# An adaLN block with windowed attention and 8 experts: rows sorted batch by batch, 13 of 39 expert tiles inside attention's drain

## What is computed

```python
mod = (_silu(L0_c) @ L0_wmod).reshape(L0_c.shape[0], 6, 1, -1)
h = _layernorm(x, axis=-1) * (1 + ca) + sa
x = x + ga * attention(h)          # 16 heads of 8, query block of 128 sees keys within +-128
h = _layernorm(x, axis=-1) * (1 + cb) + sb
router_logits = h @ gate           # [2048, 8]
routing_weights, selected = top_k(router_logits, 2); routing_weights = softmax(routing_weights)
eo[e] = (silu(h @ w1[e]) * (h @ w3[e])) @ w2[e]      # w1, w3: 128x512, w2: 512x128
x = x + gb * sum over the 2 selected experts of weight * eo[e]
```

## Time and profile before

| | us |
|---|---|
| median of 3 runs | 348.94 (348.21 to 350.21) |
| the profiled execution's own time | 349.13 |
| its span, first to last instruction | 347.3 |
| TensorE busy | 277.7 |
| VectorE busy | 227.4 |
| ScalarE busy | 184.9 |
| GpSimd busy | 180.6 |
| mean granted clock of TensorE | 0.917 |

### The profile page before, as it was taken

One profiled execution on the slowest core, in us unless ns is written; L12 is line 12 of the kernel. 1 busy time (PEld: TensorE's weight loads), 2 busy tenths in 40 slices (PEclk: granted clock), 3 DMA queues, 4 the chain that ended last, 5 costly groups with the idle time before them and its releaser, 6 DMA issues. The chain is left out here.

```text
span 347.3 us, 6884 instructions
## 1 busy us (share of the span) xinstructions
PE 277.7 (80%) x2281; PEld 204.6 (59%) x2281; DVE 227.4 (65%) x573; ACT 184.9 (53%) x406; POOL 180.6 (52%) x269
## 2 busy tenths in 40 slices
PE   3568799999998999999854056999999999999200
PEld 2134354555554555555333035999999999999200
DVE  5657978888888799887437893555555555554064
ACT  7432477757675766667710104556665555555050
POOL 4130245456655475657650125477777777775221
PEclk9999999999999999999985555999999999999855
DMA  3942332544647372300000001011111121112283
GB/s 93 175 69 60 71 100 53 175 133 141 183 109 213 73 236 67 105 1 19 17 15 16 0 0 40 23 48 54 47 47 46 53 49 46 47 46 40 78 218 92
DMA packets 36243, 26.89 MB, mean 77 GB/s; under 512 B 4088, under 2 KB 31752, under 8 KB 36208
## 3 DMA queue, kind: packets, MB, share of 16 engines
q1 hardware_dynamic: 32368, 20.48, 21.5%
q0 software_dynamic: 2496, 5.12, 5.6%
q10 hardware_dynamic: 1344, 0.86, 1.4%
HBM read 15.41 MB, written 4.67 MB: 58 GB/s over the span
## 5 line engine op out<-in xcount | busy, mean ns | idle before, releaser
L819 DVE TENSOR_REDUCE negm<-psA 128x4 f32<-128x1024 f32 x64 | 78.2, 1223 | 14.2 <-PE psA L1141 13.1
L428 ACT ACTIVATE probs<-psB 128x512 f32<-128x512 f32 x128 | 71.1, 593 | 21.4 <-PE psB L1163 21.1
L589 POOL TENSOR_SCALAR_AFFINE_SELECT probs<-probs 128x512 f32<-128x512 f32 x64 | 39.1, 634 | 42.2 <-ACT probs L428 42.2
L700 POOL DMA_INDIRECT y_d<-kd,sca_idx x39 | 45.3, 1162 | 22.9 <-ACT kd L497 22.9
L1297 PE MATMUL psA<-kd,probs 128*128 128x128 f32 x416 | 53.1, 284 | 0.0
L1297 PEld LDWEIGHTS psA<-kd,probs 128*128 128x128 f32 x416 | 51.1, 201 | 0.0
L1138 PE MATMUL psA<-kd,qs 96*128 96x512 bf16 x128 | 47.6, 395 | 1.7 <-DVE negm L819 1.5
L695 POOL DMA_INDIRECT kd<-h_d,gat_idx x39 | 38.2, 980 | 18.5 <-PE psO L1289 9.8
L1163 PE MATMUL psB<-qs,kd 98*128 98x256 bf16 x256 | 45.1, 273 | 1.5 <-ACT probs L428 1.0
L1307 PE MATMUL psM<-probs,kd 128*128 128x128 f32 x312 | 41.3, 275 | 0.4 <-ACT kd L497 0.4
L1307 PEld LDWEIGHTS psM<-probs,kd 128*128 128x128 f32 x312 | 37.9, 192 | 0.6 <-DVE kd L1030 0.6
(11 more groups left out here) (185 smaller groups left out, 402.6 us busy)
## 6 DMA issues: line engine op xcount, KB each, us to landing
w_sb<-in_L_ffn_experts_w_dram SPq DMA_DIRECT2D x12, 512.0 KB, 4.8
kd<-parts SPq DMA_DIRECT2D x96, 32.0 KB
qs<-parts SPq DMA_DIRECT2D x42, 64.0 KB
mod_sb<-mod_d SPq DMA_DIRECT2D x8, 320.0 KB, 5.0
probs<-y_d SPq DMA_DIRECT2D x8, 256.0 KB, 5.0
h_d<-h SPq DMA_DIRECT2D x8, 128.0 KB, 1.9
out_dram<-probs SPq DMA_DIRECT2D x4, 256.0 KB, 2.3
x_sb<-in_L_attn_x_dram SPq DMA_DIRECT2D x1, 640.0 KB, 9.6
```

Source lines behind the costliest of these rows:

```text
L428: nc.scalar.activation(probs[:, kt, n % PRING], psB[:, kt, :].rearrange("p (h q) -> p h q", h=H2), ACT.Exp).then_inc(s["exped"], 1)
L589: nc.gpsimd.affine_select(out=u, in_=u, compare_op=ALU.is_ge, fill=0.0, base=0, pattern=[[0, 2 * H2], [-sign, P]], channel_multiplier=sign ...
L700: pool.indirect_dma_start(y_d, bass.IndirectOffsetOnAxis(ap=sca_idx[:, n:n + 1], axis=0), ys[:, r], None).then_inc(scattered[r], 16)
L819: nc.vector.tensor_reduce(negm[:, b % 2, :, :, j], psA[:, n % 2].rearrange("p q (h k) -> p q h k", h=H2), AX.X, ALU.max, negate=True).then ...
```

## The change

- Each pair of token and expert gets its row as soon as its batch is routed. xs_d holds a region of 2176 rows for each expert: 128 blanks, then its rows in order of arrival. A row is 130 words: h2, the row of y_d for its result, and its weight. `place_rows` (VectorE) takes the ranks that `rank_rows` (TensorE) makes for two token blocks, and `put_rows` (GpSimd) writes 128 rows with one indirect DMA, four for a batch. This takes the place of the one-hot inverse and of the gathers.
- After batch 4 is routed, `early_list` makes a list of 13 tiles (NEARLY), each full and inside its region; after batch 7 `late_list` makes the other 26, counted back from each region's end.
- Steps 9 to 11 are gone. What was left of batches 5, 6 and 7 is written between the turns of the first tiles. Scatter 13 waits for the six scatters before it.
- SyncE loads a tile's rows with a plain DMA (`load_xs`, ring of 5, a slot being free when its scatter has landed) and w2 of the tile's expert from DRAM (`load_w2`); w2 is no longer held in SBUF. psG and psU have two buffers, not three.
- y_copy multiplies by the row's weight, and y_d is laid out by partition (`(k p t) c`), so that the combine is a sum.

```diff
+                sp.dma_start(pay[:, b % PAYRING, 1, :, 0:C], pay[:, b % PAYRING, 0, :, 0:C]).then_inc(h2_copied[b % PAYRING], 16)
+            def load_w2(n):
+                if n >= TRING:
+                    sp.wait_ge(s["y_ps"], n - TRING + 1)
+                e = sp.value_load(tile_e[0:1, bass.ds(n, 1)], min_val=0, max_val=E - 1)
+                sp.dma_start(w2_t[:, n % TRING].rearrange("p (k c) -> p k c", c=C),
+                             w2[bass.ds(e, 1)].rearrange("e (k p) c -> p (e k) c", p=P)).then_inc(w2_in[n % TRING], 16)
+            def load_xs(n):
+                if n >= XRING:
+                    sp.wait_ge(*result_down(n - XRING))
+                row = sp.value_load(tile_row[0:1, bass.ds(n, 1)], min_val=0, max_val=XROWS - P)
+                sp.dma_start(xs[:, n % XRING], xs_d[bass.ds(row, P), :]).then_inc(xs_in[n % XRING], 16)
...
+            sp.wait_ge(s["list_ready"], 2)
+            sp.wait_ge(s["scoresB"], 2 * NPAIR * B)
+            for n in range(TRING):
+                load_w2(n)
+            for done, count in xs_put_by(EB):
+                sp.wait_ge(done, count)
+            for n in range(XRING):
+                load_xs(n)
+            copy_h2(B - 2)
+            for n in range(NTILE):
+                if n + TRING < NTILE:
+                    if n + TRING == NEARLY:
+                        sp.wait_ge(s["list_ready"], 4)
+                    load_w2(n + TRING)
+                if n + XRING < NTILE:
+                    if n + XRING == NEARLY:
+                        sp.wait_ge(s["list_ready"], 4)
+                        sp.wait_ge(s["blanked"], 32)
+                        for done, count in xs_put_by(B):
+                            sp.wait_ge(done, count)
+                    load_xs(n + XRING)
+                if n == 2:
+                    copy_h2(B - 1)
...
+            y_t = y_d[0:TOPK * NTOK].rearrange("(k p t) c -> p k t c", k=TOPK, p=P)
             for i in range(4):
                 for k in range(TOPK):
                     sp.dma_start(y01[:, k, n * i:n * i + n], y_t[:, k, n * i:n * i + n]).then_inc(s[f"y_in{i}"], 16)
...
+            def put_rows(b, k, t):
+                r = b % PAYRING
+                pool.wait_ge(s["dest_ready"], 3 * b + 3)
+                if k == 1:
+                    pool.wait_ge(h2_copied[r], 16 * (b // PAYRING + 1))
+                pool.indirect_dma_start(xs_d, bass.IndirectOffsetOnAxis(ap=dest[:, b, k, t:t + 1], axis=0),
+                                        pay[:, r, k, t], None).then_inc(xs_put[r], 16)
...
             def scatter(n):
-                r = n % TRING
...
+                if n == NEARLY:
+                    for m in range(NEARLY - YRING, NEARLY):
+                        pool.wait_ge(*result_down(m))
                 pool.wait_ge(s["y_ready"], n + 1)
-                pool.indirect_dma_start(y_d, bass.IndirectOffsetOnAxis(ap=sca_idx[:, n:n + 1], axis=0), ys[:, r], None).then_inc(scattered[r], 16)
-            for n in range(TRING):
-                gather(n)
-            pool.wait_ge(s["xsT_first"], 1)
-            gather(TRING)
+                pool.indirect_dma_start(y_d, bass.IndirectOffsetOnAxis(ap=xs[:, n % XRING, C:C + 1].bitcast(I32), axis=0),
+                                        ys[:, n % YRING], None).then_inc(scattered[n % YRING], 16)
+            put_rows(3, 1, 1)
+            put_rows(4, 0, 0)
+            pad_term(B - 1)
+            put_rows(4, 0, 1)
+            x1_sum(B - 2)
+            put_rows(4, 1, 0)
+            ln2_rstd(B - 2)
+            put_rows(4, 1, 1)
+            h2_scale(B - 2)
+            h2_shift(B - 2)
             for n in range(NTILE):
-                if n + TRING + 1 < NTILE:
-                    pool.wait_ge(s["xsT_ps"], n + 1)
-                    gather(n + TRING + 1)
+                if n == 1:
+                    weights_pow(B - 3)
+                if n == 2:
+                    ln2_rstd(B - 1)
+                if n == 3:
+                    put_rows(B - 3, 0, 0)
+                if n == 4:
+                    weights_pow(B - 2)
+                    put_rows(B - 3, 0, 1)
+                if n == 5:
+                    weights_pow(B - 1)
+                    put_rows(B - 3, 1, 1)
+                if n == 6:
+                    put_rows(B - 2, 0, 1)
+                if n == 7:
+                    put_rows(B - 2, 1, 1)
+                if n == 8:
+                    put_rows(B - 1, 0, 1)
+                if n == 9:
+                    put_rows(B - 1, 1, 1)
                 scatter(n)
+                if n == 4:
+                    put_rows(B - 3, 1, 0)
+                if n == 5:
+                    put_rows(B - 2, 0, 0)
+                if n == 6:
+                    put_rows(B - 2, 1, 0)
+                if n == 7:
+                    put_rows(B - 1, 0, 0)
+                if n == 8:
+                    put_rows(B - 1, 1, 0)
...
+            def mix(b):
+                tt, r = slice(2 * b, 2 * b + 2), b % PAYRING
+                dve.wait_ge(s["wt_exp"], b + 1)
+                nc.vector.tensor_scalar(wts[:, 2, tt], wts[:, 1, tt], 1.0, None, ALU.add).then_inc(s["mixed"], 1)
+                dve.wait_ge(s["mixed"], 2 * b + 1)
+                nc.vector.reciprocal(pay[:, r, 0, :, C + 1], wts[:, 2, tt]).then_inc(s["mixed"], 1)
+                dve.wait_ge(s["mixed"], 2 * b + 2)
+                nc.vector.tensor_tensor(pay[:, r, 1, :, C + 1], wts[:, 1, tt], pay[:, r, 0, :, C + 1], ALU.mult).then_inc(s["dest_ready"], 1)
+            def place_rows(b):
+                dve.wait_ge(s["rank_ps"], b + 1)
+                if b >= 2:
+                    dve.wait_ge(s["dest_ready"], 3 * b - 3)
+                nc.vector.tensor_tensor(
+                    picked[:, b % 2], pick[:, :, 2 * b:2 * b + 2],
+                    rank_at(b).rearrange("p (o t e) -> p o t e", o=1, e=E).broadcast_to([P, TOPK, 2, E]), ALU.mult).then_inc(s["rank_read"], 1)
+                nc.vector.tensor_copy(pay[:, b % PAYRING, :, :, C:C + 1].rearrange("p k t o -> p k (t o)").bitcast(I32),
+                                      row_ids[:, :, 2 * b:2 * b + 2]).then_inc(s["dest_ready"], 1)
+                mix(b)
+                dve.wait_ge(s["rank_read"], b + 1)
+                nc.vector.tensor_reduce(dest[:, b], picked[:, b % 2], AX.X, ALU.max).then_inc(s["dest_ready"], 1)
...
+            def early_list():
+                dve.wait_ge(s["count_ps"], 1)
+                up_to(0, count_at(EB - 1))
+                list_done(nc.vector.tensor_scalar(jump[:], upto[:, 0, E:], -float(P), float(CAP), ALU.mult, ALU.add))
+                tile_list(0, NEARLY, jump[:])
+                list_done(nc.vector.tensor_scalar(taken[:, 0, E:], upto[:, 3, E:], float(NEARLY), None, ALU.min))
+                list_done(nc.vector.tensor_tensor(taken[:, 1, 0:E], taken[:, 0, E:], taken[:, 0, E - 1:2 * E - 1], ALU.subtract))
+            def late_list():
+                up_to(1, count_at(B - 1))
+                list_done(nc.vector.scalar_tensor_tensor(out=tile_base[:, 0:E], in0=upto[:, 3, E:], scalar=-float(P), in1=count_at(B - 1),
+                                                         op0=ALU.mult, op1=ALU.add))
+                list_done(nc.vector.tensor_scalar(tile_base[:, E:], upto[:, 3, 2 * E - 1:], -float(P), float(E * CAP), ALU.mult, ALU.add))
+                list_done(nc.vector.tensor_tensor(tile_jump[:], tile_base[:, 1:], tile_base[:, 0:E], ALU.subtract))
+                tile_list(NEARLY, NLATE, tile_jump[:])
...
+                    if j == 1 and 5 <= step < B:
+                        place_rows(step - 5)
                     if j == 1 and has(step - 3):
...
+                    if j == 0 and step == B:
+                        place_rows(3)
+                        logits_copy(4)
+                    if j == 2 and step == B:
+                        top2(4)
+                    if j == 4 and step == B:
+                        place_rows(4)
+                        early_list()
...
+            gate_attn(B - 2)
+            logits_copy(B - 3)
+            dve.wait_ge(s["list_ready"], 2)
+            dve.wait_ge(s["moe_w"], 16 * 2 * (E // 2))
+            dve.wait_ge(s["scoresB"], 2 * NPAIR * B)
+            w1_copy(0, 0)
+            w1_copy(1, 1)
+            ln2_stats(B - 2)
+            normalise_attn(B - 1)
+            ln2_normalise(B - 2)
+            top2(B - 3)
             for n in range(NTILE):
                 gate_hidden(n, n % TRING)
                 if n + 2 < NTILE:
-                    e = expert(n + 2)
-                    if n >= 1:
-                        dve.wait_ge(s["y_ps"], n)
-                    weights_copy(n + 2, (n + 2) % TRING, e)
+                    if n + 2 == NEARLY:
+                        dve.wait_ge(s["list_ready"], 4)
+                    w1_copy(n + 2, (n + 2) % TRING)
+                if n == 1:
+                    gate_attn(B - 1)
+                    x1_last(B - 1)
+                    ln2_stats(B - 1)
+                if n == 2:
```

(62 more changed lines are left out.)

495 lines of the change are left out of this document (239 added, 256 removed).

## The result

The changed kernel takes 364.39 us (median of 4 runs, 360.67 to 364.95), before 349.48 (4 runs); the ratio is 1.0408, 95% interval 1.0331 to 1.0485. The forecast was 344.5 with 336 to 353, so it is wrong in sign and outside its range. The profiled execution took 364.23 us, its span is 362.5.

What follows compares the result with a forecast made beforehand. TensorE was taken as the bound, thin only in the drain between attention and the expert tiles. +0.6 up to the late tiles and -5.0 in the combine made -4.4, so 344.5 us, range 336 to 353.

Steps and rivals of the forecast that it cites:

- attention, steps 5 to 7: Attention's later steps: place_rows on VectorE, project_out's wait for psM and GpSimd's puts add 4.0 us.
- step 8 to tile 0's transpose: End of attention: last products 6.3 us later, yet tile 0's rows arrive at 194.4 instead of 210.8, 16.4 earlier.
- T(0) to T(6): Ends of down-projections of tiles 0 to 6: 25.7 us, not 16.7, VectorE setting the time from tile 3 on.
- T(6) to T(11): Down-projection ends, tiles 6 to 11: 17.3 us, not 13.95, because tile 13's rows wait for GpSimd's last put.
- T(11) to T(38): Late tiles: nothing changes; TensorE still sets 2.79 us a tile, and xs slots and w2 reads keep up.
- combine: Final sum: longer y_d reads and weights applied in y_copy save 5.0 us.
- The largest bound given: Attention's upper bound, 8 us: TensorE waits for all of place_rows, two puts before each mask; as a rival 349, chance 0.08.
- tile 0 later than 203: Sign of being wrong: tile 0 starts later than 203 us; its transpose was expected near 198.
- one fall, at the 3.9 us of tile 6, is free: Tile 6: TensorE's clock falling once at its 3.9 us standstill costs nothing, as tile 11 waits for GpSimd anyway.
- this rival: TensorE's clock falls in the drain's tiles and stays down to tile 6: +10 us, 355 us; chance 0.08.
- the rival of the ring: Five xs slots set the tile through late scatter landings: 3.06 us a tile, 353 us in all; chance 0.17.
- late period above 2.85: Sign of being wrong: late tiles take more than 2.85 us each, where 2.79 was forecast.

Runs made afterwards that it cites:

- ranks off psM: Changed kernel with the ranks of batches 0 to 2 in a corner of psO instead of psM, puts one turn later; 352.75 us, ratio 1.0078 to before.
- the 14 fillers: Changed kernel plus 14 matmuls nobody reads on TensorE, ahead of down(6) and again ahead of tile 13's transpose; 358.12 us, ratio 1.0282 to before.
- the last kernel: Changed kernel with ranks in psO, late_list halved and later, eight xs slots, puts and loads reordered, combine's last additions on VectorE; 334.93 us, ratio 0.9572 to before.

## Why the prediction was wrong

Its sum put the span at 342.9; it is 362.5, 19.6 more. By its own terms, in us:

| term | predicted | measured | off by |
|---|---|---|---|
| attention, steps 5 to 7 | +4.0 | +11.4 | +7.4 |
| step 8 to tile 0's transpose | -16.4 | -13.7 | +2.7 |
| transpose to T(0) | +0.7 | -0.4 | -1.1 |
| T(0) to T(6) | 25.7 | 24.1 | -1.6 |
| T(6) to T(11) | 17.3 | 20.4 | +3.1 |
| T(11) to T(38) | 74.0 | 79.3 | +5.3 |
| combine | -5.0 | -1.3 | +3.7 |

**Attention is the step that failed most**, with 7.4 of the 19.6; the late tiles (5.3), the combine (3.7) and tiles 7 to 11 (3.1) are most of the rest. The prediction named the wait ("TensorE's project_out now waits for the first of them, because psM is a single buffer") and priced it by the operations inside place_rows, 1.2 a step. It should have been priced by what stands ahead of place_rows on VectorE: in step 6, 2.4 us of row maxima and 1.2 of `negmb`, hence the 2.88. The largest bound given was 8; it did not contain the clock. The run with ranks off psM regains 10.0 of 11.4. It is still not faster than before (1.0078), so attention alone did not turn the forecast's sign. The puts, 1.0 in the sum, are 2.3 by themselves. One of the prediction's own signs of being wrong came true with it: tile 0 later than 203, it was 208.5.

**Step 8** was right in its mechanism. h2_scale(5) starts 19.2 after before's, 11.5 from attention and 7.6 from the step, where 6.6 was forecast. The last put then starts 9.9 after the last product begins instead of 8.1. The prediction had the clock at full there: that product takes 3.64 at half clock, 1.93 before, and the x1 of batch 6, for which the last put waits on GpSimd, comes behind it.

**Tiles 1 to 6** were right in sum, 24.1 for 25.7, and in the stall of tile 6, 3.48 for 3.9. The parts were not: VectorE was to set the time from tile 3 on, but TensorE waits for gate_hidden only 0.50 in all before tile 6, and T(5) comes 16.7 after T(0) for 19.1. Tile 6 then takes 7.5 for 6.6, 1.0 of it down(6) at half clock. So the nearness of the sum is in part luck. But "one fall, at the 3.9 us of tile 6, is free: tile 11 waits for GpSimd anyway" was wrong, as the 14 fillers show. GpSimd's late puts stand behind scatters 6 to 8, and these wait for the tiles' results; a later tile 6 makes the puts later. What is hidden behind a queue is hidden only if that queue does not wait for it. This order is read from the program; the fillers show only that T(11) moved.

**Tiles 7 to 11**: one wait for xs at tile 13's transpose, as forecast. With the 14 fillers it was 18.2, near the 17.3; the rest of the 20.4 goes with the clock. The Trainium skill ("TensorE: Matmul & The Clock Gate", HAM oscillation — how this bites in real kernels) tells of gaps that throttle each burst anew. The trace agrees at three stalls of 2.9, 3.5 and 3.4 us. The prediction gave this rival 0.08 and looked at one place only; it was the case at several.

**Tiles 12 to 38**: half of the rival of the ring. The period is 2.79, so its rule "late period above 2.85" held in the average (79.3 / 27 = 2.94) and not in the single tile. 1.9 of the 5.3 is the half clock of tile 12, 2.1 are three waits for xs_d. The prediction's "nothing" for these tiles had no wait in it. The w2 reads landed in 2.9 in the median (2.6 to 3.7); its estimate of 2.6 used a figure for DMAs that GpSimd issues, and SyncE issues these.

**Combine**: the last operation of VectorE ends 13.8 after the first read of y_d is issued, not 10. The first pair lands 4.9 behind that, and three multiplications take 1.63, not 0.69: the prediction priced VectorE's operations as if GpSimd were silent. The kernel before shows it too: its four scaling operations of a group take 1.15 in the first and 2.14 in the third, with GpSimd's addition beside them.

## What to carry to other kernels

When a new wait is put on a shared buffer, price it by the queue of the engine that must release it, at that moment, not by the releasing instruction. Add to a stall of TensorE what the clock behind it costs, also where the stall seems covered: 2.5 us for each of two stalls of 3.5 us (fillers gave it back), and some 5 us, worked out, for three waits of 0.28, 2.88 and 1.83 in attention. A queue that mixes work for now with work for later (GpSimd's scatters and puts, SyncE's w2 and xs) has to be read as one list: the last kernel is 4.3% faster than before (some 4 us of it in the combine), but only once ranks, puts and loads no longer stood in front of what was waited for.

## What the hardware showed beside that

- VectorE is held up beside GpSimd's computing. A 128x512 multiplication takes 0.69 alone and 1.63 beside GpSimd's addition; one `before` took 0.65 beside GpSimd's x1 addition and 0.39 beside an indirect write, 0.16 alone; one `negmb` took 1.21 beside GpSimd's 1.15, 0.16 alone.
- An indirect write of 128 rows is 0.96 to 1.07 us on GpSimd (1.23 the longest) and follows the last at 1.26 to 1.38, so eight of them in a row are 10 us of that queue.
- From T(12) to T(38) the profiles differ by up to 2 us (72.5 to 74.6) with five slots of xs, though nothing was edited there, and by as much with eight (71.3 to 73.8). Terms from single profiles must not be added as if they were apart.
